# Normalising on ScalarE instead of VectorE in the three later layer norms of a two-block transformer kernel

## The chip, the cores and the metric

The kernel runs on one core of one Trainium2 chip. The metric is the device time of one execution in microseconds; the median of several runs is given. The profile is of one further execution.

## What is computed

Input x has 1,024 tokens of 256 features, all float32. Four residual steps follow one another, each behind a layer norm without weights:

```python
def _layernorm(x, axis=-1, eps=1e-05):
    m = jnp.mean(x, axis=axis, keepdims=True)
    v = jnp.var(x, axis=axis, keepdims=True)
    return (x - m) / jnp.sqrt(v + eps)
...
    x = x + attn_a(_layernorm(x), ...)   # 16 heads of 16, softmax over 1,024 tokens, LoRA projections
    x = x + ffn(_layernorm(x), ...)      # ternary weights, 256 -> 1,024 -> 256, gelu
    x = x + attn_b(_layernorm(x), ...)   # see below
    x = x + ffn(_layernorm(x), ...)
```

In attn_b a token attends over its own 16 heads, not over other tokens: for each token the scores are 16 x 16, with a causal mask over the heads, and the values enter by their sum over the features of the head.

## The kernel before

Five engines run their own instruction lists and meet at semaphores. Tokens lie on the 128 partitions, in eight tiles t of 128; two tiles make a pair p (0 to 3). The residual x stays in SBUF as `x_res[P, 8, 256]`.

The first 240 us or so hold the setup (layer norm 0, merging of the LoRA weights, projections) and seven of the eight attention units of attn_a (four heads by half of the queries each). There TensorE makes scores twice (L1185 for the row maxima, which VectorE takes at L933; L1209 for the exponentials, which ScalarE takes at L778) and multiplies by V (L1223). None of the changed code lies there: layer norm 0 keeps its form.

The rest, called the tail here, is the last attention unit, then output projection, feed-forward, attn_b and the second feed-forward, all interleaved. A planner outside of the kernel's functions gives every event a due time (`LAST_STEP`, `OUT_AT`, `FFN_AT`, `HEADS_AT` and lags behind them), sorts them into one list of 647 events, and each engine walks that list and does its own part of it in order. So an engine's order is fixed, and an instruction that waits holds all that stand behind it on its engine. For a norm the events are

- `var` (k, p): VectorE's bn_stats and bn_aggr for two tiles, then variance + eps into `rstd` (L877 to L884), then on GpSimd the power -0.5 (L617);
- `norm`: the normalised pair `xn`, a buffer of two pairs, 1.78 us of plan later;
- `lnt`: TensorE's four transposes (L1131, in `transpose_pair`);
- `lnt_out`: ScalarE's evacuation (L695 or L814, `evacuate_lnt` or `first_x_part`), and `x_rest` on VectorE (L1018, `second_x_part`).

Layer norm k = 1 stands ahead of the first feed-forward, 2 ahead of attn_b, 3 ahead of the second feed-forward. Their twelve norms run at 260.66, 266.40, 285.20, 291.30 (k = 1), 295.36, 306.47, 325.69, 342.32 (k = 2), 343.83, 370.29, 403.42 and 419.86 us (k = 3).

What else stands in the engines' lists in the tail:

- ScalarE: the last exponentials (L778), `o_out` (L809), `gelu` (L823), `qk_out` (L829), `vs_out` (L833), `exp_heads` (L837). Gelu and Exp need different tables, and a load stands between them.
- VectorE: residuals (L979, L997), the second part of gelu (`g_rest`, L1025), head sums (`sum`, L1036, a reduction of GpSimd's products), the softmax over heads (`soft`, L1042 to L1044, and `wv`, L1051 to L1058).
- GpSimd: the power (L617), the third part of gelu (`g3`, L654), the products of q and k of a token's heads in four sizes (`prod`, L666).

ScalarE's list around the norms that the change moves to it: exponential 25, norm (1,0), exponentials 26 and 27, evacuation of (1,0), exponentials 28 to 31, norm (1,1), evacuation of (1,1), then the first gelu. Norms (1,2), (1,3) and (2,0) each stand ahead of a gelu that the same list held back to back with others before. Norm (3,1) stands ahead of `qk_out` of tile 5. Norm (3,3) stands ahead of the second gelu of its range.

Of the kernel before, what the change touches and what calls it, by code (L numbers as in the profile page):

```python
# [31 lines left out]
ALU = mybir.AluOpType  # L32
ACT = mybir.ActivationFunctionType
AX_X = mybir.AxisListType.X

P = 128
T, D, H, HD, RANK, FF = 1024, 256, 16, 16, 16, 1024
TT = T // P
PAIRS = TT // 2
# [192 lines left out]
def numbered():  # L232

    of, count = {}, {}
    events = [(kind, 0, p) for kind in ("var", "norm", "lnt") for p in range(PAIRS)]
    for e in [*events, *tail_events()]:
        of[e] = count.get(e[0], 0)
        count[e[0]] = of[e] + 1
    return of
# [46 lines left out]
def build(nc, a):  # L286
    uses, base = plan_banks()
    number = numbered()
    events = list(tail_events())
    norms = [e for e in number if e[0] == "norm"]  # L290
# [3 lines left out]
    with ExitStack() as ctx:  # L294
        def sb(name, shape, dt=F32):
            return ctx.enter_context(nc.sbuf_tensor(name, shape, dt))

        def sem(name):
            return ctx.enter_context(nc.semaphore(name))


        x_res = sb("x_res", [P, TT, D])
        xn = sb("xn", [P, 2, 2, D])
# [54 lines left out]
        stats = sb("stats", [P, TT, 6])  # L358
        mv = sb("mv", [P, TT, 2])
        rstd = sb("rstd", [P, TT])  # L360
        minus_half = sb("minus_half", [P, 2])
        abs_sum = sb("abs_sum", [P, 2])
        thr = sb("thr", [P, 2, 2])
# [43 lines left out]
        stats_ready = sem("stats_ready")  # L407
        rstd_ready = sem("rstd_ready")
        xn_ready = sem("xn_ready")
        rest_ready = sem("rest_ready")  # L410
        part_ready = sem("part_ready")
        parts_out = [sem(f"parts_out{i}") for i in range(6)]
# [42 lines left out]
        def is_filled(eng, key):  # L455
            b, n = uses[key]
            eng.wait_ge(filled[b], n + 1)
            return ps[:, b, :]
# [8 lines left out]
        def drain_sem(key):  # L467
            return drained[uses[key][0]]
# [212 lines left out]
        def _(act):  # L681
# [79 lines left out]
            def evacuate_pv(g, qh, u):  # L761
                act.wait_ge(filled[PV_BANK], base[PV_BANK] + u + 1)
                act.copy(o_un[:, bass.ds(g, 1), HALF * qh:HALF * qh + HALF].rearrange("p g t -> p (g t)"),
                         ps[:, PV_BANK, :]).then_inc(drained[PV_BANK], 1)

            def exp_tile(u, s):
                c, j = divmod(s, G)
                place = ring_place(s, isinstance(u, int) and u == NU - 1)
                i = place % len(SCORE_BANKS)
                b = SCORE_BANKS[i]  # L770
                act.wait_ge(filled[b], base[b] + u * RING_USES + ring_fills(place, i))
                if j == 0 and not (isinstance(u, int) and u == 0 and c < 2):

                    if c == 1:
                        act.wait_ge(filled[PV_BANK], base[PV_BANK] + u)
                    else:
                        act.wait_ge(pv_chunk, u * (TT - 1) + (c - 1 if c else 0))
                act.activation(pbuf[:, c % 2, j, :], ps[:, b, :], ACT.Exp).then_inc(drained[b], 1)  # L778
# [29 lines left out]
            def o_out(key):  # L808
                act.copy(oT[:, number[key] % 2, :, :], is_filled(act, key)[:, 0:D].rearrange("p (c t) -> p c t", c=DC)) \  # L809
                    .then_inc(drain_sem(key), 1)  # L810

            def first_x_part(k, p):
                src = is_filled(act, ("lnt", k, p)).rearrange("p (c t) -> p c t", c=DC)
                act.mul(x12[:, 0, :, 256 * p:256 * p + 256], src, X_SCALE).then_inc(x1_ready, 1)  # L814

            def gelu(key):
                _, r, s, f = key
                src = is_filled(act, key)[:, 0:RANGE]
                n = len(RANGES[0]) * r + s
                if f == 0 and n >= KEPT:  # L820
                    old_r, old_s = divmod(n - KEPT, len(RANGES[0]))
                    is_filled(act, ("y", old_r, RANGES[old_r][old_s][0] // 2))
                act.activation(g_full[:, kept(r, s), f, :], src, ACT.Gelu, bias=b1_col[:, f:f + 1]) \  # L823
                    .then_inc(drain_sem(key), 1)

            def qk_out(t):
                if t >= 3:
                    act.wait_ge(divided, t - 2)
                act.copy(qk[:, t % 3, :, :].rearrange("p h n -> p (h n)"), is_filled(act, ("qk", t))) \  # L829
                    .then_inc(drain_sem(("qk", t)), 1)  # L830

            def vs_out(t):
                act.copy(v_sum[:, t % 3, :], is_filled(act, ("vs", t))[:, 0:HD]).then_inc(drain_sem(("vs", t)), 1)  # L833

            def exp_heads(t):
                act.wait_ge(shifted, t + 1)
                act.activation(probs[:, t % 2, :, :], probs[:, t % 2, :, :], ACT.Exp, scale=SCALE).then_inc(exped, 1)  # L837

            for e in events:
                if e[0] == "exp":  # L840
                    exp_tile(NU - 1, e[1])
                if e[0] == "pv_out":
                    evacuate_pv(NG - 1, 1, NU - 1)
                if e[0] == "o_out":
                    o_out(("o", *e[1:]))
                if e[0] == "lnt_out":
                    (evacuate_lnt if e[1] == 2 else first_x_part)(*e[1:])
                if e[0] == "gelu":
                    gelu(("h", *e[1:]))
                if e[0] == "qk_out":  # L850
                    qk_out(e[1])
                if e[0] == "vs_out":
                    vs_out(e[1])
                if e[0] == "exp_heads":
                    exp_heads(e[1])
# [5 lines left out]
        def _(dve):  # L861
# [11 lines left out]
            def variances(k, p):  # L873
                if k == 0:
                    dve.wait_ge(x_in[p], 16)
                for t in (2 * p, 2 * p + 1):
                    dve.bn_stats(stats[:, t, :], x_res[:, t, :]).then_inc(dve_step, 1)  # L877
                    steps[0] += 1
                dve.wait_ge(dve_step, steps[0])
                for t in (2 * p, 2 * p + 1):  # L880
                    dve.bn_aggr(mv[:, t, :], stats[:, t, :]).then_inc(dve_step, 1)
                    steps[0] += 1
                dve.wait_ge(dve_step, steps[0])
                dve.tensor_scalar(rstd[:, 2 * p:2 * p + 2], mv[:, 2 * p:2 * p + 2, 1], EPS, None, ALU.add) \  # L884
                    .then_inc(stats_ready, 1)

            def normalise(k, p):
                n = number["norm", k, p]
                dve.wait_ge(rstd_ready, number["var", k, p] + 1)
                if n >= 2:  # L890
                    is_filled(dve, ("lnt", *norms[n - 2][1:]))
                for i in (0, 1):
                    t = 2 * p + i
                    ins = dve.tensor_scalar(xn[:, n % 2, i, :], x_res[:, t, :], mv[:, t, 0:1], rstd[:, t:t + 1],  # L894
                                            ALU.subtract, ALU.mult)
                ins.then_inc(xn_ready, 1)
# [86 lines left out]
            def ternary_out(n):  # L983

                c, key = n // 2, ("w", n)
                src = is_filled(dve, key).bitcast(BF16)
                if n % 2 == 0:
                    dve.tensor_scalar(w1T[:, c, :], src, 1.0 / X_SCALE, None, ALU.mult).then_inc(drain_sem(key), 1)
                else:
                    dve.tensor_copy(w2T[:, 4 * c:4 * c + 4, :].rearrange("p f d -> p (f d)"), src) \  # L990
                        .then_inc(drain_sem(key), 1)
# [78 lines left out]
            for e in events:  # L1070
                if e[0] == "w":
                    ternary_out(e[1])
                if e[0] == "div":
                    divide(("ao_t", e[1]))
                if e[0] == "res":
                    r, t = e[1:]
                    residual(r, t, ("ao_y", t) if r == 0 else ("bo_y", t))
                if e[0] == "res_pair":
                    residual_pair(*e[1:])
                if e[0] == "var":  # L1080
                    variances(*e[1:])
                if e[0] == "norm":
                    normalise(*e[1:])
                if e[0] == "x_rest":
                    second_x_part(*e[1:])
                if e[0] == "g_rest":
                    gelu_rest(*e[1:])
                if e[0] == "sum":
                    head_scores(e[1], e[2])
                if e[0] == "soft":  # L1090
                    soften(e[1])
                if e[0] == "wv":
                    head_outputs(e[1])
# [348 lines left out]
```

## Time and profile before

| | |
|---|---|
| median of 3 runs | 446.09 us (444.82 to 447.0) |
| the profiled execution, its own time | 444.14 us |
| its span, first to last instruction | 442.3 us |
| mean granted TensorE clock | 0.954 |
| TensorE busy | 387.7 us, 88% |
| VectorE busy | 334.3 us, 76% |
| ScalarE busy | 234.2 us, 53% |
| GpSimd busy | 151.5 us, 34% |

In the profile PE is TensorE, DVE is VectorE, ACT is ScalarE and POOL is GpSimd; L894 is line 894 of the kernel before. A share of busy time is a mean over the whole span. An entry such as [0.58 <-POOL rstd L617] says how long the engine sat idle before the instruction and what ended the idle time.

### The profile page before, as it was taken

The page shows a single profiled execution, that of the slowest core. Times are in us where ns is not written, and L with a number is a line of the kernel's source. Part 1 is how long each engine was busy: PE and PEld are TensorE (multiplying, and loading weights), DVE is VectorE, ACT ScalarE, POOL GpSimd, SP SyncE. Part 2 cuts the span into 40 slices and gives each one's busy share as a digit, 9 for nine tenths or more (in the row PEclk, how much of TensorE's full clock was granted, in tenths as well). Part 3 has the DMA queues.
Part 4 walks back from the last instruction along what each step waited for, and adds up shares of the span by engine and source line. Part 5 has one row for each costly group of instructions (what it writes and reads, how often), then busy time and mean ns, then how long its engine had stood idle before and what let it go on. Part 6 is the DMA issues. An engine that isn't in the chain of part 4 may idle for free.

```text
span 442.3 us, 6344 instructions
## 1 busy us (share of the span) xinstructions
PE 387.7 (88%) x2132; PEld 186.0 (42%) x2132; DVE 334.3 (76%) x511; ACT 234.2 (53%) x452; POOL 151.5 (34%) x159
## 2 busy tenths in 40 slices
PE   2999797989999999999998998988987599486597
PEld 1644342222222232222222444775764265344385
DVE  6538699888878788888882445686899989999643
ACT  2156323668776877677778756232541263264232
POOL 4025207995000000000000003355795848666153
PEclk9999897999999999999999999999898689789899
DMA  7708984940000000000000000000000000000001
GB/s 206 218 2 216 247 227 83 177 77 0 3 1 1 0 0 1 0 1 0 1 0 3 1 1 1 0 1 0 2 2 0 0 0 1 24 0 2 24 1 47
DMA packets 12644, 17.42 MB, mean 39 GB/s; under 512 B 4391, under 2 KB 10443, under 8 KB 11950
## 3 DMA queue, kind: packets, MB, share of 16 engines
q1 hardware_dynamic: 10862, 15.95, 15.1%
q10 hardware_dynamic: 1760, 1.18, 0.8%
q8 instruction: 13, 0.21, 0.2%
q14 instruction: 9, 0.07, 0.1%
HBM read 12.73 MB, written 4.19 MB: 38 GB/s over the span
## 4 chain that ended last, share of the span: by engine, by line
PE 58%; DVE 26%; ACT 5%; DMA 4%; issue 4%; POOL 1%; SPq 1%; ACTq 0%; DVEq 0%
PE ps L1223 14%; PE ps L1209 13%; PE ps L1185 12%; DVE s_raw L1036 5%; PE ps L1356 4%; DVE xn L894 3%; DVE pack L1025 3%; PE ps L1345 2%; PE ps L1330 2%; DVE parts L1053 2%; DVE mx L933 2%; PE ps L1131 2%; DVE stats L877 2%; DVE parts L1042 2%; DMA pack<-q_parts 2%
## 5 line engine op out<-in xcount | busy, mean ns | idle before, releaser
L933 DVE TENSOR_REDUCE mx<-ps 128x1 f32<-128x1024 f32 x128 | 151.2, 1221 | 30.3 <-PE ps L1185 29.8
L778 ACT ACTIVATE pbuf<-ps 128x512 f32<-128x512 f32 x256 | 136.1, 605 | 51.9 <-PE ps L1209 51.1
L1185 PE MATMUL ps<-pack 112*128 (+1 forms) x256 | 79.3, 393 | 4.5 <-DMA pack<-q_parts 2.8
L1209 PE MATMUL ps<-pack 115*128 (+1 forms) x256 | 81.8, 387 | 0.8 <-ACT pbuf L778 0.8
L617 POOL TENSOR_TENSOR rstd<-rstd,minus_half 128x2 f32<-128x2 f32 x16 | 12.1, 757 | 196.8 <-DVE rstd L884 196.7
L1223 PE MATMUL ps<-pbuf,v_slot 128*32 128x512 f32 x512 | 68.2, 604 | 2.1 <-ACT pbuf L778 0.9
L1209 PEld LDWEIGHTS ps<-pack 115*128 (+1 forms) x256 | 21.2, 97 | 80.7 <-issue 61.1
L666 POOL TENSOR_TENSOR pbuf<-wT 128x1024 f32<-128x1024 f32 (+3 forms) x32 | 50.9, 1600 | 11.8 <-ACT wT L829 8.7
L1356 PE MATMUL ps<-w_nat,pack 128*128 128x256 bf16 x384 | 51.8, 278 | 2.6 <-POOL pack L654 2.4
L654 POOL TENSOR_TENSOR pack<-pack 128x256 bf16<-128x256 f32 x64 | 42.3, 671 | 26.8 <-DVE pack L1025 26.8
L1025 DVE TENSOR_TENSOR pack<-pack 128x256 f32<-128x256 f32 x64 | 33.8, 538 | 14.2 <-ACT pack L823 14.0
L1356 PEld LDWEIGHTS ps<-w_nat,pack 128*128 128x128 bf16 x384 | 37.1, 100 | 12.9 <-POOL pack L654 4.7
L1345 PE MATMUL ps<-v_sb,w_nat 128*128 128x256 f16 x256 | 40.2, 295 | 1.7 <-DVE v_sb L1018 1.4
L823 ACT ACTIVATE pack<-ps,b_col 128x256 f32<-128x256 f32 x64 | 29.0, 477 | 23.0 <-PE ps L1345 22.6
L1185 PEld LDWEIGHTS ps<-pack 112*128 (+1 forms) x256 | 22.6, 99 | 32.4 <-DVE mx L933 7.6
L1345 PEld LDWEIGHTS ps<-v_sb,w_nat 128*128 128x128 f16 x256 | 26.9, 106 | 9.0 <-issue 2.2
L1036 DVE TENSOR_REDUCE s_raw<-pbuf 128x64 f32<-128x1024 f32 (+3 forms) x32 | 25.3, 808 | 0.0
L894 DVE TENSOR_SCALAR xn<-x_res,mv,rstd 128x256 f32<-128x256 f32 x32 | 20.6, 685 | 1.9 <-POOL rstd L617 1.2
L1223 PEld LDWEIGHTS ps<-pbuf,v_slot 128*32 128x32 f32 x512 | 10.1, 107 | 26.3 <-ACT pbuf L778 17.0
L809 ACT COPY parts<-ps 128x256 f32<-128x256 f32 x16 | 6.0, 376 | 28.0 <-PE ps L1318 28.0
L1318 PE MATMUL ps<-ident,parts 128*128 128x128 f32 x32 | 7.0, 303 | 15.6 <-DVE parts L1058 15.6
L646 POOL TENSOR_SCALAR below<-w_nat,thr 128x512 bf16<-128x512 f32 x8 | 12.6, 1570 | 21.6 <-DVE thr L955 21.0
(114 smaller groups left out, 414.4 us busy)
## 6 DMA issues: line engine op xcount, KB each, us to landing
pack<-q_parts SPq DMA_DIRECT2D x6, 384.0 KB, 14.4
w_nat<-in_L_ffn_w_dram SPq DMA_DIRECT2D x2, 1024.0 KB, 6.9
k_parts<-parts SPq DMA_DIRECT2D x2, 768.0 KB, 7.3
q_parts<-parts SPq DMA_DIRECT2D x4, 384.0 KB, 8.9
pack<-k_parts SPq DMA_DIRECT2D x4, 384.0 KB, 7.2
pack<-k_parts SPq DMA_DIRECT2D x2, 768.0 KB, 9.4
x_res<-in_L_attn_a_x_dram SPq DMA_DIRECT2D x4, 256.0 KB, 3.7
out_dram<-x_res SPq DMA_DIRECT2D x4, 256.0 KB, 2.2
```

What stands on the lines that cost most here:

```text
L654: pool.tensor_tensor(g_low[:, k, f, :], g_left[:, k, f, :], g_mid[:, k, f, :, 1], ALU.subtract) \
L666: pool.tensor_tensor(out, in0, in1, ALU.mult).then_inc(products, 1)
L778: act.activation(pbuf[:, c % 2, j, :], ps[:, b, :], ACT.Exp).then_inc(drained[b], 1)
L894: ins = dve.tensor_scalar(xn[:, n % 2, i, :], x_res[:, t, :], mv[:, t, 0:1], rstd[:, t:t + 1], ALU.subtract, ALU.mult)
L933: dve.tensor_reduce(mx[:, par, k:k + 1], ps[:, b:b + 2, :].rearrange("p b k -> p (b k)"), AX_X, ALU.max) \
L1025: dve.tensor_tensor(g_left[:, k, f, :], g_full[:, k, f, :], g_top[:, k, f, :, 1], ALU.subtract).then_inc(g_rest, 1)
L1036: dve.tensor_reduce(s_raw[:, t % 2, i, 0:nj], terms, AX_X, ALU.add).then_inc(reduced, 1)
L1185: ins = pe.matmul(ps[:, b + n, :], q_group[0:ROWS, qh, at, j, P * qt:P * qt + P].rearrange("p g t -> p (g t)"), k_group[0:ROWS, at, j, HAL ...
L1209: pe.matmul(ps[:, b, :], k_group[0:SROWS, at, j, P * c:P * c + P].rearrange("p g t -> p (g t)"), q_group[0:SROWS, qh, at, j, :].rearrange( ...
L1223: ins = pe.matmul(ps[32 * j:32 * j + 32, PV_BANK, :], v_slot[:, qh, c, j, :], pbuf[:, c % 2, j, :], start=(c == 0), stop=(c == TT - 1))
L1345: ins = pe.matmul(out, w1T[:, c, P * f:P * f + P], x12[:, part, c, v], start=(part == 0 and c == 0), stop=(part == 1 and c == DC - 1))
L1356: ins = pe.matmul(out, part, w2T[:, f, :], start=False, stop=(f == FC - 1 and n == NPART - 1 and i == 1))
```

## The change

For k = 1, 2, 3 the `norm` event moves from VectorE's list to ScalarE's, at the same place in the order. VectorE additionally writes the negated means of a pair, `less_mean`, between bn_aggr and the variance. ScalarE waits for `rstd`, multiplies `less_mean` by it for each of the two tiles (`offset`), waits for these two, and applies an Identity activation with scale `rstd` and bias `offset`, one column of each per token tile. The wait for the buffer of `xn` and the count on `xn_ready` stay as they were.

```diff
@@ -358,6 +358,8 @@
         rstd = sb("rstd", [P, TT])
+        less_mean = sb("less_mean", [P, TT])
+        offset = sb("offset", [P, TT])
@@ -407,6 +409,7 @@
         xn_ready = sem("xn_ready")
+        offset_ready = sem("offset_ready")
@@ -809,6 +812,19 @@
+            def normalise(k, p):
+                n = number["norm", k, p]
+                act.wait_ge(rstd_ready, number["var", k, p] + 1)
+                for t in (2 * p, 2 * p + 1):
+                    act.mul(offset[:, t:t + 1], less_mean[:, t:t + 1], rstd[:, t:t + 1]).then_inc(offset_ready, 1)
+                is_filled(act, ("lnt", *norms[n - 2][1:]))
+                act.wait_ge(offset_ready, 2 * (n - PAIRS) + 2)
+                for i in (0, 1):
+                    t = 2 * p + i
+                    ins = act.activation(xn[:, n % 2, i, :], x_res[:, t, :], ACT.Identity, bias=offset[:, t:t + 1],
+                                         scale=rstd[:, t:t + 1])
+                ins.then_inc(xn_ready, 1)
@@ -843,6 +859,8 @@
+                if e[0] == "norm":
+                    normalise(*e[1:])
@@ -881,6 +899,8 @@
                 dve.wait_ge(dve_step, steps[0])
+                if k:
+                    dve.tensor_scalar(less_mean[:, 2 * p:2 * p + 2], mv[:, 2 * p:2 * p + 2, 0], -1.0, None, ALU.mult)
                 dve.tensor_scalar(rstd[:, 2 * p:2 * p + 2], mv[:, 2 * p:2 * p + 2, 1], EPS, None, ALU.add) \
                     .then_inc(stats_ready, 1)
@@ -1079,8 +1099,6 @@
-                if e[0] == "norm":
-                    normalise(*e[1:])
```

## Rows read from the trace of the kernel before

**Rows 1.** The page: busy time of each engine (part 1), chain by line (part 4).
```profile
PE 387.7 (88%) x2132; PEld 186.0 (42%) x2132; DVE 334.3 (76%) x511; ACT 234.2 (53%) x452; POOL 151.5 (34%) x159
...
PE ps L1223 14%; PE ps L1209 13%; PE ps L1185 12%; DVE s_raw L1036 5%; PE ps L1356 4%; DVE xn L894 3%; DVE pack L1025 3%; PE ps L1345 2%; PE ps L1330 2%; DVE parts L1053 2%; DVE mx L933 2%; PE ps L1131 2%; DVE stats L877 2%; DVE parts L1042 2%; DMA pack<-q_parts 2%
```

**Rows 2.** Windows 299 to 417 us: length, VectorE busy (instructions), clock; then L894 alone.
```profile
299.00:417.00 118.00, 103.74 (x185) 0.88 0.02 5
...
299.00:417.00 118.00, 11.84 (x12) 0.88 0.02 5
```

**Rows 3.** Groups by line and form, 255 to 443 us: busy us, mean ns | idle before.
```profile
L1025 DVE TENSOR_TENSOR pack<-pack 128x256 f32<-128x256 f32 x64 | 33.8, 538 | 14.2 <-ACT pack L823 14.0
...
L894 DVE TENSOR_SCALAR xn<-x_res,mv,rstd 128x256 f32<-128x256 f32 x24 | 17.7, 777 | 1.2 <-POOL rstd L617 1.2
...
L823 ACT ACT_TABLE_LOAD x8 | 10.3, 1283 | 0.1
...
L837 ACT ACTIVATE parts<-parts 128x256 f32<-128x256 f32 x8 | 3.3, 418 | 13.1 <-DVE parts L1044 13.1
...
L884 DVE TENSOR_SCALAR rstd<-mv 128x2 f32<-128x2 f32 x12 | 2.4, 203 | 0.4
```

**Rows 4.** The normalising line in the last 188 us: duration ns min/median/max, first and last start.
```profile
L894 DVE TENSOR_SCALAR xn<-x_res,mv,rstd x24: 396/697/2411, 260.7 to 420.5; 128x256 f32<-128x256 f32 x24
```

**Rows 5.** Time line of all engines, 295 to 411 us, single instructions.
```profile
295.98 0.83 PE L1356 MATMUL ps<-w_nat,pack 128*128 128x256 bf16 x6 [1.27 <-POOL pack L654]
...
306.47 3.02 DVE L894 TENSOR_SCALAR xn<-x_res,mv,rstd 128x256 f32<-128x256 f32 x2 [0.58 <-POOL rstd L617]
...
306.98 2.37 POOL L666 TENSOR_TENSOR pbuf<-wT 128x1024 f32<-128x1024 f32 x1
...
309.93 1.98 POOL L666 TENSOR_TENSOR pbuf<-wT 128x768 f32<-128x768 f32 x1
...
311.49 0.70 DVE L1025 TENSOR_TENSOR pack<-pack 128x256 f32<-128x256 f32 x1 [1.24 <-ACT pack L823]
...
343.25 1.99 POOL L666 TENSOR_TENSOR pbuf<-wT 128x512 f32<-128x512 f32 x2
...
346.34 0.43 DVE L1042 TENSOR_TENSOR parts<-s_raw,causal 128x256 f32<-128x256 f32 x1
...
403.42 2.51 DVE L894 TENSOR_SCALAR xn<-x_res,mv,rstd 128x256 f32<-128x256 f32 x2
...
407.77 0.72 POOL L666 TENSOR_TENSOR pbuf<-wT 128x256 f32<-128x256 f32 x1
...
410.30 0.42 DVE L1042 TENSOR_TENSOR parts<-s_raw,causal 128x256 f32<-128x256 f32 x1
```

**Rows 6.** Time line, VectorE, 418 to 421 us.
```profile
418.50 0.25 DVE L881 BATCH_NORM_AGGREGATE mv<-stats 128x2 f32<-128x6 f32 x2
...
419.86 1.01 DVE L894 TENSOR_SCALAR xn<-x_res,mv,rstd 128x256 f32<-128x256 f32 x2 [0.58 <-POOL rstd L617]
```

**Rows 7.** Time line, ScalarE, 23 to 44 us: start, us, instruction [idle before].
```profile
23.29 0.21 ACT L729 ACTIVATE kq_bias<-kq_bias 128x2 f32<-128x2 f32 x1
26.55 0.69 ACT L719 ACTIVATE cut<-ps,kq_bias 128x512 f32<-128x512 f32 x1 [3.06 <-PE ps L1144]
27.14 0.68 ACT L720 ACTIVATE parts<-ps,kq_bias 128x512 bf16<-128x512 f32 x1
...
42.71 0.59 ACT L706 COPY wT<-ps 128x512 f32<-128x512 f32 x1
```

**Rows 8.** Time line, ScalarE and TensorE, 262 to 269 us.
```profile
262.61 0.60 ACT L778 ACTIVATE pbuf<-ps 128x512 f32<-128x512 f32 x1 [0.22 <-PE ps L1209]
264.54 0.60 ACT L778 ACTIVATE pbuf<-ps 128x512 f32<-128x512 f32 x1 [1.33 <-PE ps L1209]
...
265.51 2.08 ACT L778 ACTIVATE pbuf<-ps 128x512 f32<-128x512 f32 x4
...
268.64 0.66 PE L1131 MATMUL ps<-ident,xn 128*128 128x128 f32 x4
```

## The prediction

> **What bounds the kernel now.** I read the page first, then the groups of instructions of the last 188 us by form, then the time line around each of the twelve norms that the change touches. The page shows TensorE busy 88% of the span and VectorE 76%, ScalarE only 53% [rows 1]. That is an average over two regimes. The attention units, up to about 240 us, are untouched. In the rest the reader should look at VectorE between 299 and 417 us: 103.7 of 118 us busy [rows 2]. There it looks like the bound, and the chain of work puts 3% of the span, 13 us, on the line that the change takes off it [rows 1].
>
> The second thing to see is the duration of that line. The 24 instructions take 396 ns at least, 697 in the median and 2,411 at most, for one shape [rows 3, 4]. The subtraction of two SBUF tensors (L1025) averages 538 [rows 3]. At 306.47 two norms take 3.02 us, and the second ends as GpSimd's 2.37 us product ends; at 311.49 a subtraction waits in the same way for the product begun at 309.93 [rows 5]. So some VectorE instructions stand still until the running GpSimd instruction is over. Of 24 x 777 = 18.6 us on the line [rows 3], 24 x 0.41 = 9.8 are work and 8.8 such waiting. What matters for the change: a wait for GpSimd isn't removed with the instruction that shows it, if the next VectorE instruction with the same habit takes its place.
>
> **What the change removes.** 24 tensor_scalar instructions of VectorE, in twelve pairs, 0.73 to 0.75 us a pair where nothing disturbs it.
>
> **What it adds on VectorE.** Twelve tensor_scalar instructions 128x2, ahead of the variance that GpSimd waits for. One alone has 0.20 us [rows 3]; two small ones in a row take 0.25 together [rows 6], so the second adds at most 0.12. Bounds 0 and 0.20; I take 0.10, as nothing waits for it alone. I reckon with seven of the twelve on the path: +0.7 us (at 0.20: 1.4).
>
> **What it adds on ScalarE.** Per pair, two 128x1 multiplications, a wait for them, two 128x256 activations. The nearest small one is 0.21 us, with an immediate scale [rows 7]. An operand per partition costs 0.10: L719 with a bias column is 0.69, L706, a copy of the same size, 0.59 [rows 7]; consecutive instructions start 0.59 apart where one has 0.69, an overlap of 0.10 [rows 7]. Small ones: 0.21 + 0.10 = 0.31, and 0.21 more for the second, 0.52. The large: 0.42 from SBUF with an immediate scale [rows 3], plus two columns, 0.62; the second 0.52 more, 1.14. With 0.04 for the wait, 1.7 us a pair. Bounds: 1.1 (no price for columns: 0.17 for the second small one at most, 0.42 + 0.32 for the large) and 1.9 (no overlap). I take 1.7, since the column's price is seen on this engine. The Trainium skill, "ScalarE: Activation LUTs", What ACT_TABLE_LOAD costs, gives 186 ns + 0.833 ns an element + 93 ns per column operand and 93 ns of overlap, an estimate of 1.55 us a pair; by that the sum below would be 0.4 lower. The same page, Rules for kernel authors, sends additions and multiplications to VectorE; that speaks against the change, and the rows agree in size: 1.7 for 0.73 undisturbed. So the path from the inverse deviation to the normalised tile grows by 1.0 us, wherever VectorE was at hand at once and undisturbed. ScalarE has room: twelve pairs add 20 us to an engine idle for 47% of the span. But it works in order: what stands behind a norm waits for the variance, GpSimd's power, and 1.7 us.
>
> Now norm by norm; (k, p) is layer norm k, pair p.
>
> (1,0) and (1,1), beside the last attention unit. ScalarE's order puts norm (1,0) ahead of the exponential at 262.61. Before that it is idle from 262.39, so the norm holds it until 264.1, and that exponential comes 1.5 us late. The next one, at 264.54, was itself waiting 1.33 us for scores [rows 8], which takes up 1.1; 0.4 remains. Four exponentials then keep ScalarE busy until 267.6 [rows 8], norm (1,1) stands behind them, and its tile is ready 2.1 us later than 267.6 including the delay, at 269.7. The transposes that used to run at 268.64 [rows 8] start 1.05 us late, and ScalarE's evacuation, table load and first gelu follow them. +1.05.
>
> (1,2), (1,3), (2,0), 285 to 299 us. TensorE leads here; the one larger gap, 1.27 us at 295.98, waits for GpSimd's third part [rows 5], itself behind a power that waits for VectorE. VectorE loses a norm ahead of it (1.0) but waits longer for a gelu queued behind ScalarE's norm (0.6). -0.2.
>
> (2,1), 3.02 us on VectorE at 306.47, and (2,2), the same pattern. It looks like the large gain. But ScalarE hands the tile over at 308.7 (0.8 early), the gelu after it comes at 310.6, and the subtraction that needs it then meets GpSimd's product of 309.93 to 311.9, as it did before, and ends at 312.2, as before [rows 5]. The wait is shifted from the norm to its neighbour. 0 (bound: -0.8 each).
>
> (2,3), (3,0), around 343 us. The head sums behind them can't end before GpSimd's products, 343.25 + 1.99 = 345.24, plus 0.4; VectorE ended them at 346.31 and L1042 began at 346.34 [rows 5]. It can begin at 345.7, of which half is lost again to products later on: -0.35. (3,1): GpSimd works without a gap there, 0.
>
> (3,2), 2.51 us at 403.42. ScalarE is idle, and hands over at 404.3, 1.6 early. The last product of this group begins at 407.77 and has 0.72 [rows 5]; the scores could be finished 0.7 after that, at 409.2, where L1042 began at 410.30. -1.1.
>
> (3,3), the last, 1.01 us at 419.86 [rows 6]. TensorE waits for it and is the bound from there to the end; 1.7 in its place, +0.7.
>
> Sum: 1.05 - 0.2 + 0 - 0.35 - 1.1 + 0.7 + 0.7 = +0.8. Against the profiled execution, 444.14 us (span 442.3), this makes 444.9; the median of the runs is 446.09, 1.95 above, so 446.9.
>
> A rule on the waits: "SBUF — State Buffer", Who interferes with whom, in the Trainium skill, says that tensor_scalar in its 2-port mode and instructions with two SBUF inputs contend with GpSimd for one port pair, that the other side blocks wholly, and that ScalarE never does. The trace agrees on VectorE [rows 3, 5]; that ScalarE's new instructions keep their time beside products no row of before shows. Were they held like VectorE's, (2,1) alone would lose over a microsecond.
>
> **The rivals.**
> *VectorE's relief gets through.* For it: 88% busy between 299 and 417, and 13 us of chain on the line [rows 1, 2]. Six pairs have 11.84 us there [rows 2]. A path that runs through VectorE's list alone gains all of it; one through the tile gains 11.84 - 6 x 1.7 = 1.6. The middle is 6.7, with 0.4 for the first stretch 7.1, less 2.45 of additions (1.05 + 0.7 + 0.7) -4.65: 441.4. Against it: the ends that coincide with GpSimd's. It holds if VectorE, being early, gets in ahead of a product instead of behind it.
>
> *ScalarE's queue becomes the wait (slower).* Place: the five norms up to 299 us, where TensorE has hardly a gap. Gelus behind norms (1,2), (1,3), (2,0) come 1.7 to 2.5 us late. I have them covered by subtractions that VectorE only reaches later. If the cover is gone in two of the three, 2 x 1.7 = 3.4 and the -0.2 and the -0.35 are lost too: 446.9 + 3.95 = 450.9. It decides where a late gelu exceeds the slack of about 1.5 us.
>
> *Extra table loads.* If Identity weren't in Gelu's table, some eight norms would stand between two loads of 1.28 us [rows 3]: 20 us, 467. L719 is an Identity too and runs without a load, though not after a gelu [rows 7]. "ScalarE: Activation LUTs" in the Trainium skill, Table sets, says that identity is in every set; by that no load comes.
>
> **How the numbers follow.** Half a per cent, 2.2 us, is about what a measurement can tell from no change. Forecast near zero 0.46; relief gets through, wholly or half, 0.29; queue 0.22; table loads 0.03. The near-zero case spreads over 444 to 448.3, by the bounds 1.1 and 1.9 on three exposed norms (-1.8, +0.6), 0.7 on the small instruction, and 0.8 for (2,1). The range reaches to just inside both rivals: 441.8 to 450.2. Faster 0.30, same 0.46, slower 0.24.
>
> **What would show it.** L894 keeps its 8 instructions of the first norm; new activations of 0.62 and 0.31 us, no new loads. The transposes of (1,1) about 1 us later, those of (3,2) about 1.5 earlier relative to their variance. L1025's mean above 538, L1053 and L1042 not shorter: the waits moved. Idle time of VectorE up by nearly what left it. I am wrong if L1025 stays at 538 and VectorE's stretch shrinks by several microseconds, or if TensorE's gaps before 299 us grow by over 2.

## The result and the profile after

| | before | after |
|---|---|---|
| median | 445.43 us (20 runs, 442.45 to 448.45) | 447.86 us (20 runs, 445.5 to 449.18) |
| ratio | | 1.0048, 95% interval 1.0027 to 1.0068 |
| the profiled execution, own time | 444.14 us | 448.24 us |
| its span | 442.3 us | 446.4 us |

By the ratio the change costs about 2.1 us, by the two medians 2.4. Forecast were +0.8 us and 446.9 us, and 444 to 448.3 us for the case near zero. The measured 447.86 us lies in that band and the sign is right, but the loss is over twice the forecast one, and the way to it held one misjudged place.

The page of the changed kernel, parts 1 and 4:

```profile
PE 388.8 (87%) x2132; PEld 186.1 (42%) x2132; DVE 320.0 (72%) x499; ACT 251.3 (56%) x500; POOL 151.0 (34%) x159
...
PE ps L1241 14%; PE ps L1227 13%; PE ps L1203 11%; PE ps L1374 4%; DVE mx L953 3%; DVE s_raw L1056 3%; PE ps L1363 3%; DVE pack L1045 2%; PE ps L1348 2%; DVE parts L1073 2%; PE ps L1149 2%; ACT xn L824 2%; POOL pbuf L669 2%; ACT pbuf L781 2%; DMA pack<-q_parts 1%
```

Against [rows 1] VectorE has 14.3 us less and ScalarE 17.1 us more. The normalising line had 3% of the chain on VectorE; now 2% stand on ScalarE's L824, and GpSimd's products (L669), absent from the list before, have 2%.

The groups of the tail by form, to be read beside [rows 3]:

```profile
L1045 DVE TENSOR_TENSOR pack<-pack 128x256 f32<-128x256 f32 x64 | 34.4, 547 | 26.1 <-ACT pack L839 26.1
...
L824 ACT ACTIVATE xn<-x_res,offset,rstd 128x256 f32<-128x256 f32 x24 | 13.1, 593 | 1.1
...
L819 ACT ACTIVATE offset<-less_mean,rstd 128x1 f32<-128x1 f32 x24 | 5.8, 293 | 11.2 <-POOL rstd L620 11.2
...
L903 DVE TENSOR_SCALAR less_mean<-mv 128x2 f32<-128x2 f32 x12 | 2.4, 202 | 0.4
...
L1073 DVE TENSOR_TENSOR parts<-parts,hsum 128x256 f32<-128x256 f32 x8 | 9.9, 1233 | 0.3
...
L1062 DVE TENSOR_TENSOR parts<-s_raw,causal 128x256 f32<-128x256 f32 x8 | 6.9, 862 | 0.3
```

The last two in the kernel before:

```profile
L1053 DVE TENSOR_TENSOR parts<-parts,hsum 128x256 f32<-128x256 f32 x8 | 10.1, 1260 | 0.3
...
L1042 DVE TENSOR_TENSOR parts<-s_raw,causal 128x256 f32<-128x256 f32 x8 | 6.7, 838 | 0.3
```

A small activation takes 293 ns, a large one 593; on the time line two small ones are over in 0.48 us, two large ones in 1.09 (below). From the end of GpSimd's power to the tile that makes 1.69 us, where 1.7 was worked out. The negation has 0.20 us, and the variance begins 0.07 after it. The subtraction in the second part of gelu (L1045), which shares VectorE's list with the norms, went from 538 to 547 ns, in a second trace of the changed kernel to 539. What rose is VectorE's idle time ahead of it, waiting for ScalarE's gelu: from 14.2 us [rows 3] to 26.1.

VectorE's window from 299 to 417 us (length, busy, instructions, clock):

```profile
299.00:417.00 118.00, 94.62 (x180) 0.88 0.01 3
```

It was 103.74 us [rows 2]. So 9.1 us left the stretch that looked VectorE-bound, and the stretch didn't get shorter. To see where they went, take the starts of TensorE's four transposes of each pair in the time line, counted from those of (1,0), since the setup ahead differs by up to 2.3 us from run to run:

| pair | (1,1) | (1,2) | (1,3) | (2,0) | (2,1) | (2,2) | (2,3) | (3,0) | (3,1) | (3,2) | (3,3) | end |
|---|---|---|---|---|---|---|---|---|---|---|---|---|
| before | 4.95 | 24.10 | 28.89 | 33.05 | 45.86 | 64.31 | 80.09 | 81.75 | 108.41 | 142.30 | 157.24 | 178.6 |
| after | 5.55 | 24.70 | 29.49 | 33.26 | 45.08 | 63.22 | 81.37 | 84.20 | 110.83 | 143.33 | 159.75 | 182.5 |
| late | 0.60 | 0.60 | 0.60 | 0.21 | -0.78 | -1.09 | 1.28 | 2.45 | 2.42 | 1.03 | 2.51 | 3.9 |

The zero of this table moves itself. Against the matmuls of the projection ahead of them, the transposes of (1,0) come 0.30 us later in the changed kernel (1.27 us behind their start, before 0.97). Before, then after:

```profile
262.72 1.13 PE L1330 MATMUL ps<-wT,parts 128*128 128x256 f32 x4
263.69 0.60 PE L1131 MATMUL ps<-ident,xn 128*128 128x128 f32 x4
```

```profile
262.62 1.13 PE L1348 MATMUL ps<-wT,parts 128*128 128x256 f32 x4
263.89 0.66 PE L1149 MATMUL ps<-ident,xn 128*128 128x128 f32 x4
```

So 0.3 us are to be added to each number of the last row. The traces of all versions below show the 1.27 wherever norm (1,0) runs on ScalarE at full width, and the 0.97 everywhere else.

The reader sees a small loss at (1,1), a lead up to (2,2), and a jump of 3.5 us over the next two pairs. Here is that place in the changed kernel, all engines, single instructions:

```profile
339.64 2.08 PE L1348 MATMUL ps<-w_out,parts 128*128 128x256 f32 x4
...
342.18 3.24 PE L1409 MATMUL ps<-w_nat,xT 128*128 128x512 f32 x4
...
343.60 0.69 POOL L620 TENSOR_TENSOR rstd<-rstd,minus_half 128x2 f32<-128x2 f32 x1 [1.01 <-DVE rstd L904]
...
345.26 0.60 PE L1149 MATMUL ps<-ident,xn 128*128 128x128 f32 x4
...
345.89 0.59 ACT L698 COPY xT<-ps 128x512 f32<-128x512 f32 x1 [3.37 <-PE ps L1149]
346.38 0.48 ACT L819 ACTIVATE offset<-less_mean,rstd 128x1 f32<-128x1 f32 x2
346.95 1.09 ACT L824 ACTIVATE xn<-x_res,offset,rstd 128x256 f32<-128x256 f32 x2
...
348.09 1.09 PE L1149 MATMUL ps<-ident,xn 128*128 128x128 f32 x4 [2.23 <-ACT xn L824]
...
350.37 2.33 POOL L669 TENSOR_TENSOR pbuf<-wT 128x1024 f32<-128x1024 f32 x1 [4.18 <-ACT wT L845]
```

The power of (3,0) ends at 344.29. ScalarE starts on the norm only at 346.38, since in its list the evacuation of (2,3) stands ahead (L698, 345.89), and this waits for TensorE's transposes of (2,3), which stand behind two long groups of matmuls (339.64 and 342.18). The tile of (3,0) comes at 348.04 instead of the 345.98 that the power would allow. `qk_out` stands behind it in turn, and GpSimd sits idle for 4.18 us until 350.37. On VectorE, before, the norm depended on nothing but the power and VectorE's own list.

The jump has three parts of about 1.2 us each. The lead of 1.09 at (2,2) is gone by the next output projection (its transposes, L1336, come at 74.27 where L1318 had 74.18). From there to the transposes of (2,3) TensorE takes 7.1 us instead of 5.9; its granted clock is the lower one for more of that stretch, a mean of 0.56 of 2.4 GHz against 0.68, after an idle time of 2.65 us against 2.38. And from (2,3) to (3,0) it takes 2.83 us instead of 1.66, which is the norm's place in ScalarE's list. TensorE's windows from the projection's bias to the transposes of (2,3), before and after:

```profile
338.98:344.30 5.32, 5.32 (x14) 0.68 0.00 0
```

```profile
339.32:345.42 6.10, 6.10 (x12) 0.56 0.00 0
```

### The profile page after: what moved, and what is told of

It is laid out like the page before. It is cut to its first block, busy times and chain, and to the rows that moved or that the text cites. A ratio compares the mean times of both kernels' runs of the same rounds, so it can differ in the third digit from the quotient of the medians.

```text
span 446.4 us, 6380 instructions
## 1 busy us (share of the span) xinstructions
PE 388.8 (87%) x2132; PEld 186.1 (42%) x2132; DVE 320.0 (72%) x499; ACT 251.3 (56%) x500; POOL 151.0 (34%) x159
## 4 chain that ended last, share of the span: by engine, by line
PE 58%; DVE 21%; ACT 8%; POOL 4%; DMA 4%; issue 3%; SPq 1%; ACTq 0%; DVEq 0%
PE ps L1241 14%; PE ps L1227 13%; PE ps L1203 11%; PE ps L1374 4%; DVE mx L953 3%; DVE s_raw L1056 3%; PE ps L1363 3%; DVE pack L1045 2%; PE ps L1348 2%; DVE parts L1073 2%; PE ps L1149 2%; ACT xn L824 2%; POOL pbuf L669 2%; ACT pbuf L781 2%; DMA pack<-q_parts 1%
## 5 line engine op out<-in xcount | busy, mean ns | idle before, releaser
L1374 PE MATMUL ps<-w_nat,pack 128*128 128x256 bf16 x384 | 50.4, 273 | 6.1 <-POOL pack L657 6.1
L669 POOL TENSOR_TENSOR pbuf<-wT 128x1024 f32<-128x1024 f32 (+3 forms) x32 | 50.6, 1590 | 13.8 <-ACT wT L845 10.7
L1045 DVE TENSOR_TENSOR pack<-pack 128x256 f32<-128x256 f32 x64 | 34.4, 547 | 26.1 <-ACT pack L839 26.1
L1374 PEld LDWEIGHTS ps<-w_nat,pack 128*128 128x128 bf16 x384 | 36.1, 98 | 16.9 <-POOL pack L657 9.3
L839 ACT ACTIVATE pack<-ps,b_col 128x256 f32<-128x256 f32 x64 | 29.0, 474 | 22.9 <-PE ps L1363 22.6
L1203 PEld LDWEIGHTS ps<-pack 112*128 (+1 forms) x256 | 22.8, 100 | 32.6 <-issue 7.8
L1336 PE MATMUL ps<-ident,parts 128*128 128x128 f32 x32 | 7.3, 314 | 17.3 <-DVE parts L1078 17.3
L649 POOL TENSOR_SCALAR below<-w_nat,thr 128x512 bf16<-128x512 f32 x8 | 12.6, 1570 | 22.8 <-DVE thr L975 22.1
L1149 PE MATMUL ps<-ident,xn 128*128 128x128 f32 x64 | 12.7, 336 | 7.5 <-ACT xn L824 7.3
```

What stands on the lines that cost most here:

```text
L669: pool.tensor_tensor(out, in0, in1, ALU.mult).then_inc(products, 1)
L1045: dve.tensor_tensor(g_left[:, k, f, :], g_full[:, k, f, :], g_top[:, k, f, :, 1], ALU.subtract).then_inc(g_rest, 1)
L1203: ins = pe.matmul(ps[:, b + n, :], q_group[0:ROWS, qh, at, j, P * qt:P * qt + P].rearrange("p g t -> p (g t)"), k_group[0:ROWS, at, j, HAL ...
L1374: ins = pe.matmul(out, part, w2T[:, f, :], start=False, stop=(f == FC - 1 and n == NPART - 1 and i == 1))
```

## The experiments

Each was run in rounds beside the kernel before, on the same chip; the ratio is to that.

| version | norms on ScalarE | ratio (95%) | median us |
|---|---|---|---|
| changed kernel again | all 12 | 1.0043 (1.0016 to 1.0071) | 447.61 |
| all_but_30 | all but (3,0) | 0.9997 (0.9969 to 1.0025) | 445.82 |
| early_30 | all 12, (3,0) earlier in the list | 0.9963 (0.9927 to 0.9999) | 443.66 |
| three | (2,1), (2,2), (3,2) | 0.9962 (0.9938 to 0.9987) | 444.58 |
| few_dve | none; 8 of 256 columns on VectorE | 0.9982 (0.9950 to 1.0015) | 444.25 |
| few_act | all 12, 8 of 256 columns | 0.9994 (0.9965 to 1.0023) | 444.51 |
| only_k1 | (1,0) to (1,3) | 1.0047 (1.0019 to 1.0075) | 446.57 |
| six | (2,1) to (3,2), (3,0) earlier | 0.9985 (0.9952 to 1.0018) | 444.51 |
| six again | the same | 1.0008 (0.9981 to 1.0035) | 445.18 |
| only_30 | (3,0) | 1.0062 (1.0032 to 1.0091) | 446.46 |
| only_33 | (3,3) | 1.0089 (1.0056 to 1.0123) | 447.82 |
| short_prod | none; short products | 0.9644 (0.9606 to 0.9683) | 427.93 |

The medians of before beside them were 445.32 (first four), 444.7 (next four) and 443.98 (last four). Three theories stood against each other after the comparison of the traces: the loss is one norm's place in ScalarE's list (queue theory); it is the longer path of every norm (hand-over theory); it is TensorE's lower granted clock after 338 us (clock theory).

**The changed kernel again.**

> The changed kernel as it is, on the chip of the next three. All theories: 1.005 of before, 2 us slower.

1.0043, and the transposes lie within 0.15 us of the first trace in every column. The loss repeats.

**Norm (3,0) back on VectorE.** A set `ON_ACT` names the pairs; VectorE's and ScalarE's tiles are counted on a semaphore each.

```diff
-                if e[0] == "norm":
+                if e[0] == "norm" and e[1:] in ON_ACT:
                     normalise(*e[1:])
```

> Norm (3,0) back on VectorE, the other eleven on ScalarE. Queue theory (most of the loss is norm (3,0) standing in ScalarE's list behind the evacuation of (2,3), which waits for TensorE): the transposes of (3,0) come some 2 us earlier than in the changed kernel, and the time falls by 2, to 1.000 of before (0.999 to 1.002). Hand-over theory (each of the twelve costs about the same by its longer path): one twelfth of the loss back, 1.0044. Clock theory (TensorE's lower granted clock after 338 us, which the place of this norm doesn't touch, is most of it): 1.004.

0.9997. The transposes of (3,0) stand at 81.82 instead of 84.20, those of (3,1) at 108.25 instead of 110.83. Moving one norm of twelve takes back the whole loss; the 1.0044 of the hand-over theory lies outside the interval. The clock theory's 1.004 does too, but it assumed that the norm's place doesn't touch the clock, and here TensorE's window ahead of the transposes of (2,3) has 0.68 again, as before. The next version tells the two apart.

```profile
339.50:344.90 5.40, 5.34 (x13) 0.68 0.00 0
```

**The order of two entries in ScalarE's list.**

```diff
-            for e in events:
+            mine = list(events)
+            mine.remove(("norm", 3, 0))
+            mine.insert(mine.index(("lnt_out", 2, 3)), ("norm", 3, 0))
+            for e in mine:
```

> All twelve on ScalarE, and in ScalarE's list alone norm (3,0) stands ahead of the evacuation of (2,3) instead of behind it. Queue theory: the norm runs as soon as the power is there, about 344.3 to 346.0, the transposes of (3,0) start at 346.1 and not 348.1, time falls by 1.5 to 2 us: 1.001 of before. Hand-over theory and clock theory: no change against the changed kernel, 1.005.

0.9963, more than expected and barely clear of 1. The same instructions on the same engines; ScalarE, TensorE and GpSimd in the time line of this version:

```profile
342.94 0.48 ACT L819 ACTIVATE offset<-less_mean,rstd 128x1 f32<-128x1 f32 x2 [1.60 <-POOL rstd L620]
343.51 1.09 ACT L824 ACTIVATE xn<-x_res,offset,rstd 128x256 f32<-128x256 f32 x2
...
344.23 1.08 PE L1152 MATMUL ps<-ident,xn 128*128 128x128 f32 x8
...
346.51 5.68 POOL L669 TENSOR_TENSOR pbuf<-wT 128x1024 f32<-128x1024 f32 x3 [1.69 <-ACT wT L845]
```

The norm starts as soon as its power is there. TensorE finds both pairs ready and runs eight transposes in one go at 344.23, and GpSimd's next product comes at 346.51 after a short wait instead of 4.18 us. (2,3) itself is as late as in the changed kernel, 81.51; with (3,0) ready in time this costs nothing, as (3,1) shows: 108.17 against 108.41 before. TensorE's clock in the stretch ahead was 0.52 here, lower still than the 0.56 of the changed kernel, so the lower clock alone isn't the loss; it makes (2,3) late, and the order of the list decides whether (3,0) inherits that.

```profile
337.90:344.30 6.40, 6.37 (x11) 0.52 0.00 0
```

The two orders differ by 2.6 us at the last transposes (157.18 and 159.75) and by 3.95 us in the medians. Against before, the trace shows no gain (the last transposes 0.07 us early in the table's count, 0.2 late with the 0.3 of (1,0)); the measured 0.9963 goes with a higher mean clock in its runs, 0.952 against 0.946.

**Three norms on ScalarE.**

> Only norms (2,1), (2,2), (3,2) on ScalarE, the three longest on VectorE; the other nine stay on VectorE. If VectorE's relief mostly meets GpSimd's products again: only (3,2) counts, -1 us, 0.997 to 0.999 of before. If the relief gets through wherever ScalarE is idle: 3.0 + 2.3 + 2.5 us of VectorE time, at least -4 us, 0.991. Hand-over theory: +0.5 us, 1.001.

0.9962: -1.7 us, between the first two cases. By the trace (3,2)'s transposes come 1.28 us earlier than before (141.02), and (2,1), (2,2) 1.0 and 1.3 earlier, of which nothing is left at (3,1) (108.50). The eight microseconds that VectorE loses here bring under two, so neither "only (3,2) counts" nor "at least 4 us" is met exactly; the first is nearer.

**Few columns, on either engine.** Both leave out the normalising of columns 8 to 255 in the three later layer norms.

```diff
-                    ins = dve.tensor_scalar(xn[:, n % 2, i, :], x_res[:, t, :], ...)
+                    c = slice(0, 8 if k else D)
+                    ins = dve.tensor_scalar(xn[:, n % 2, i, c], x_res[:, t, c], ...)
```

> The kernel before, but VectorE normalises only the first 8 of 256 columns in the three later layer norms (the rest of the buffer keeps what layer norm 0 left; this leaves out most of the normalising). It takes 12 to 15 us of VectorE's time away at no cost elsewhere, with the queues as before. If a wait for GpSimd's products is shifted to the neighbour: 2 to 4 us faster, 0.991 to 0.996 of before, and L1025 and L1053 average more than 538 and 1260 ns. If VectorE's relief gets through: 8 us or more, below 0.983, and L1025 stays.

0.9982, no measurable gain, and the premise of both cases failed: VectorE's busy time fell by 2.7 us in all (334.3 to 331.6), not by 12 to 15. The means of the neighbours didn't rise either (L1025's place 537 ns, L1053's 1,262). Its line in that version (minimum, median, maximum in ns):

```profile
L895 DVE TENSOR_SCALAR xn<-x_res,mv,rstd x24: 276/576/2370, 261.1 to 420.8; 128x8 f32<-128x8 f32 x24
```

A thirty-second of the columns, and the maximum is 2,370 ns against 2,411 [rows 4]. Minimum and median fell by 0.12 us each, from 396 and 697; so much is the price of 248 columns, the rest of the shortest is there whatever the width, and what lies above it is waiting. The version therefore didn't test what VectorE's relief is worth.

> The changed kernel, but ScalarE normalises only the first 8 columns (the same part is left out). The two activations take about 0.4 us in place of 1.1, the place in ScalarE's list stays. Queue theory: the norm (3,0) still stands behind the evacuation of (2,3), so its transposes stay over 1.5 us later than in the kernel with few columns on VectorE; against the changed kernel 12 x 0.7 less where exposed, about 2 us, 1.000 of before. Hand-over theory (the longer instructions are the loss): all of the loss and more goes, 0.995 or less, equal to the few columns on VectorE.

0.9994, as the queue theory expected (1.000), while the hand-over theory's 0.995 lies just outside the interval. ScalarE's line has no such waits (mean in ns):

```profile
L824 ACT ACTIVATE xn<-x_res,offset,rstd 128x8 f32<-128x8 f32 x24 | 8.1, 385 | 1.1
```

The gap between the transposes of (2,3) and (3,0) stays 2.42 us (78.60 and 81.02), where few columns on VectorE leave 0.63 (80.96 and 81.59). So the place in the list holds the norm back whatever its length. But the queue theory's other number failed: the transposes of (3,0) are not over 1.5 us later than with few columns on VectorE, they are 0.57 earlier, since those of (2,3) come 2.4 earlier. The shorter path is felt: the last transposes stand 4.3 us earlier than in the changed kernel (155.47 against 159.75). The place isn't all of the loss; it is the part that could be taken off by itself.

**Only layer norm 1.**

> Only the four norms of layer norm 1 on ScalarE. By the terms of the prediction +1.05 at (1,1) and -0.2 after it, 0.1 for the small instruction: +0.9, by the changed kernel's own trace +0.6 at the transposes of (1,1): 1.001 to 1.003 of before. ScalarE's queue as the wait in the stretch up to 299 us (late gelus): +3 us or more, 1.007.

1.0047. The interval, 1.0019 to 1.0075, overlaps the first expectation at its lower end only, and holds the 1.007 of the queue as well. In the trace the loss is +0.60 at (1,1), +0.53 at (2,0) and stays at that up to (3,2); +0.88 at (3,3). With the 0.3 us of (1,0) that is 0.9 at (1,1), as expected. Late gelus add nothing after (1,1), so the trace doesn't bear out ScalarE's queue up to 299 us. Four norms measure as large a loss as all twelve; up to (3,3) the trace has 1.2 of the measured 2.1 us, and what makes the rest is open.

**Six norms.** The list's change of early_30 with `ON_ACT` from (2,1) to (3,2).

> On ScalarE: (2,1), (2,2), (2,3), (3,0), (3,1), (3,2), with (3,0) ahead of the evacuation of (2,3); (1,p), (2,0) and (3,3) stay on VectorE. It leaves out the exposed places (1,1) and (3,3) and the queued one. Expected 0.995 to 0.998 of before, as the version with three. If VectorE's relief adds up with the number of norms taken off: 0.992.

> The version with six norms on ScalarE, (3,0) ahead of the evacuation, a second time, since its first interval (0.9952 to 1.0018) told nothing apart. By the trace its last transposes stand 1.9 us earlier than before's against the first ones: 0.996. If what VectorE loses is worth nothing: 1.000.

0.9985 and 1.0008. The last transposes stand 1.9 us earlier than before's in both traces (155.30, 155.29), but the time doesn't follow measurably. Of the two, "what VectorE loses is worth nothing" is closer.

**Only (3,0), only (3,3).**

> Only norm (3,0) on ScalarE, at its place behind the evacuation of (2,3). Queue theory: it starts when that evacuation ends, its tile comes some 1.4 us later than on VectorE, more where TensorE runs at the lower clock ahead of it; 1.003 to 1.006 of before. Hand-over theory: the tile comes 0.2 to 1.0 later, VectorE has 1.5 us less: 1.000.

1.0062. The transposes of (3,0) come 1.25 us later than before (83.00 against 81.75), where 1.4 was expected. A single norm costs at its place what the queue theory says, and the measured 2.5 us (difference of the medians) are more than the trace has. The mean clock of these runs is 0.939 against 0.950 beside them; what of the difference goes with the clock can't be told apart.

> Only the last norm, (3,3), on ScalarE. Its path is exposed: 1.7 us in place of 1.0, and 0.1 for the small instruction: transposes 0.8 later, 1.002 of before (1.000 to 1.004 with the measurement). If the lower clock that follows the longer wait of TensorE comes on top, 1.004.

1.0089, above both numbers. The trace has +0.86 from (3,2) to (3,3), as expected; another 1.3 us arise at (2,3), ahead of the moved norm, where this version has the same instructions as before. They come from TensorE's clock: behind the transposes of (2,2) its granted clock is 0.79 in the mean over 8 us where before had the full one in the same place. TensorE's idle time ahead of it was the same, 1.26 and 1.25 us. Before, then this version, from 62.0 us of the table on:

```profile
325.69:333.69 8.00, 6.75 (x45) 1.00 0.01 2
```

```profile
324.05:332.05 8.00, 6.74 (x34) 0.79 0.01 2
```

Another 1.6 us lie behind the last transposes, of which more below. So one norm alone measures more than all twelve, and the losses of only_k1, only_30 and only_33 don't add up to that of the changed kernel: single versions carry a difference of a microsecond or two that isn't their norm's.

**Short products.** GpSimd multiplies 2 of 16 features; the other terms are left out.

> The kernel before, but GpSimd's products over the heads cover only 2 of 16 features (the rest of the products is left out, the sums read what stands in the buffer). If the long durations of VectorE's normalising line are waits for these products: its maximum falls from 2,411 ns to below 1,000, its mean from 777 to about 450, L1053's from 1260 to about 430, and the kernel gets 8 us or more faster, since 50 us of GpSimd's work go and with them some 15 us of waits. If they are something else, the durations stay.

0.9644, 16 us faster. VectorE's lines in this version, mean and then minimum, median, maximum:

```profile
L894 DVE TENSOR_SCALAR xn<-x_res,mv,rstd 128x256 f32<-128x256 f32 x24 | 11.6, 524 | 1.2 <-POOL rstd L617 1.2
...
L1053 DVE TENSOR_TENSOR parts<-parts,hsum 128x256 f32<-128x256 f32 x8 | 3.5, 439 | 0.3
...
L894 DVE TENSOR_SCALAR xn<-x_res,mv,rstd x32: 396/411/752, 5.9 to 401.3; 128x256 f32<-128x256 f32 x32
```

The maximum fell from 2,411 to 752 ns, the mean from 777 to 524, L1053's from 1,260 to 439. The long durations were waits for GpSimd's products. What of the 16 us VectorE's waits were is not shown, since the products themselves stand on the tail's path too. The mean stayed above the 450 expected, since GpSimd's third part of gelu (L654) still stands in the way.

## Why the prediction was right, point by point

**The number.** The direction was forecast, and the time lies in the band near zero, partly by luck. The rise was forecast as 0.8 us and measured as 2.1. The forecast time was nearer than the rise because it stood on a median of 3 runs, 446.09 us, where 20 runs give 445.43. And the stated range, 441.8 to 450.2 us, would have held the median of every version above except short_prod.

**"The waits moved".** Right at one place, (2,1), wrong in sum. I had expected L1025's mean above 538 ns and L1053 and L1042 not shorter. Measured were 547 and, in the second trace, 539 ns; 1,233 against 1,260; 862 against 838. These three lines together gained 0.6 us of busy time, where 8.8 us of waiting had been reckoned on the norms. Most of that wait left VectorE's instructions and became idle time ahead of L1045, 11.9 us more. VectorE's idle time rose from 108.0 to 126.4 us, as expected: by the 14.3 us that left it and the longer span. So its relief ended for the most part in waits for ScalarE's gelus, and only at single places in waits for GpSimd.

**The price of a norm on ScalarE.** Worked out 1.7 us, measured 1.69; small 0.31, measured 0.29. Right. No table load was added (L839 has 8 in the tail, as L823 had).

**(1,0) and (1,1), +1.05.** Right: +0.90, that is 0.60 by the table and the 0.30 of (1,0). ScalarE's list in the changed kernel and TensorE:

```profile
267.69 0.51 ACT L819 ACTIVATE offset<-less_mean,rstd 128x1 f32<-128x1 f32 x2
268.30 1.09 ACT L824 ACTIVATE xn<-x_res,offset,rstd 128x256 f32<-128x256 f32 x2
...
269.44 0.66 PE L1149 MATMUL ps<-ident,xn 128*128 128x128 f32 x4 [0.47 <-ACT xn L824]
```

The norm starts behind the exponentials at 267.69 and TensorE waits 0.47 us for it. Of the delay brought in by norm (1,0), 0.4 had been reckoned. Counted from the matmuls ahead (262.62, before 262.72), the exponential that stood at 264.54 comes 0.36 late, at 264.80.

**(1,2), (1,3), (2,0), -0.2.** -0.39 (0.60 to 0.21). Right: gelus behind these norms made VectorE wait, but TensorE took no harm.

**(2,1) and (2,2), 0.** Right, to 0.3 us. This was the step on which the forecast differed from "VectorE is the bound", and the trace follows it to the instruction:

```profile
307.83 1.09 ACT L824 ACTIVATE xn<-x_res,offset,rstd 128x256 f32<-128x256 f32 x2
...
308.97 0.66 PE L1149 MATMUL ps<-ident,xn 128*128 128x128 f32 x4 [1.09 <-ACT xn L824]
...
310.55 1.80 POOL L669 TENSOR_TENSOR pbuf<-wT 128x768 f32<-128x768 f32 x1
...
310.66 1.98 DVE L1045 TENSOR_TENSOR pack<-pack 128x256 f32<-128x256 f32 x1 [2.83 <-ACT pack L839]
...
317.92 0.43 DVE L1062 TENSOR_TENSOR parts<-s_raw,causal 128x256 f32<-128x256 f32 x1
```

The transposes are 0.8 us early, the subtraction begins at 310.66, right behind the start of a product at 310.55, and takes 1.98 us to 312.64. The scores of the tile (L1062) begin at 317.92, which counted from (1,0) is 54.03 against 53.78 before: nothing of three microseconds is left. Behind (2,2) the scores of the next tile are 0.3 us early.

**(2,3) and (3,0), -0.35.** This step failed. I had placed the norms by the power and by GpSimd's products and had not asked what stands ahead of norm (3,0) in ScalarE's list. From the transposes of (2,2) to those of (3,0) the lateness grew by 3.5 us, where it should have shrunk; from the scores of the tile ahead (67.94 against 68.25, at the second L1062) by 2.8. At the row that the forecast named, L1042 at 346.34, the scores came 0.14 us late (82.79 against 82.65) instead of 0.35 early. The large loss is at the tile after it, whose `qk_out` stands behind norm (3,0): 97.28 against 94.65. With only the order of two entries changed, (3,0) stands 0.2 us late (early_30, 81.95). In the changed kernel it stands 2.45 us late. Part of that comes from TensorE's slower stretch ahead of (2,3), which was not in the sum either. The rival "ScalarE's queue becomes the wait" had the right mechanism and the wrong place, the stretch up to 299 us.

**(3,1), 0.** -0.03. **(3,2), -1.1.** -1.39 at the transposes, of which 0.43 is gone by the next projection (L1336, 8.70 us later against 8.27): -0.96. Right.

**(3,3), +0.7.** From L1336 to the transposes 7.72 us against 6.67, of which 0.33 is a slower output projection; +0.72 for the norm. Right. ScalarE and TensorE:

```profile
421.93 0.48 ACT L819 ACTIVATE offset<-less_mean,rstd 128x1 f32<-128x1 f32 x2 [1.35 <-POOL rstd L620]
422.50 1.09 ACT L824 ACTIVATE xn<-x_res,offset,rstd 128x256 f32<-128x256 f32 x2
...
423.64 1.11 PE L1149 MATMUL ps<-ident,xn 128*128 128x128 f32 x4 [2.73 <-ACT xn L824]
424.55 1.92 PE L1363 MATMUL ps<-v_sb,w_nat 128*128 128x256 f16 x8
```

What follows on TensorE was not in the sum. Its matmuls behind the transposes take 1.92 us for eight where before had 1.04; the granted clock of the stretch is 0.72 of 2.4 GHz, a mean between the two levels, where before kept the full one; TensorE had stood idle for 2.73 us ahead of these transposes, before for 2.00. The windows of TensorE, 420 to 432 us, after and before (clock in the fourth place):

```profile
420.00:432.00 12.00, 9.27 (x66) 0.72 0.01 1
```

```profile
420.00:432.00 12.00, 11.07 (x98) 1.00 0.01 1
```

That is 1.4 us from (3,3) to the end (22.8 against 21.4). It isn't a fair part of the loss, though: all other versions with whole products have 22.7 to 24.3 there, few_dve with the same order of instructions as before too. That the trace of before is a lucky one here is likely, not shown: there is one trace of it, and its 444.14 us are 1.3 below the median of 20. The lateness at (3,3), 2.5 us by the table and 2.8 with the 0.3 of (1,0), is the better account, and lies near the ratio's 2.1.

**The negation, +0.7.** Too large: 0.07 us a pair, 0.5 for the seven reckoned. They are part of the differences above and can't be told apart.

## What to carry to other kernels

Before an instruction is moved to an idle engine, read what stands ahead of it in that engine's list and what those entries wait for; idle time there is often waiting that the newcomer joins, and a swap of two entries can be worth more than the move. An instruction whose duration varies sixfold at one shape is waiting: look for what ends when it ends. Taking it away can pass the wait to the next instruction of that kind, as at (2,1), or turn it into idle time behind another engine, as in most places here; in neither case is its busy time a gain. And a trace has to be counted from a point ahead of everything that the change touches; the first moved norm is already too late.

## What the runs showed of the hardware

A tensor_scalar of 128x8 on VectorE took up to 2,370 ns beside GpSimd's products, while an activation on ScalarE kept its time. Its 24 instructions in the changed kernel (minimum, median, maximum in ns), four pairs of which ran beside products of 1.8 to 2.6 us:

```profile
L824 ACT ACTIVATE xn<-x_res,offset,rstd x24: 584/593/601, 262.7 to 423.0; 128x256 f32<-128x256 f32 x24
```

"SBUF — State Buffer", Who interferes with whom, in the Trainium skill, says that VectorE and GpSimd share a port pair which one of them holds for a whole instruction while the other is blocked, and that ScalarE never waits on anyone. The durations here agree with both.

The kernel before itself varies by 6 us, and its time goes with the mean granted clock of TensorE, the longer runs having the lower one: over the 35 runs beside the first four versions the two correlate with -0.85, over the next 34 with -0.74, over the last 23 with -0.71 (worked out from each run's time and clock). Which of the two is the cause these numbers don't show. A difference of half a per cent, 2.2 us, is about a third of this spread, and single traces differ by over 1 us in stretches of equal instructions.
